# Preparing a bidirectional state-space layer: the step-size chain on 128 rows, the running sums split once, and the input stack and projections by token halves

## The reference

```python
def _mamba3(x, in_proj, conv_w, conv_b, A_log, dt_bias, D, norm_w, out_proj):
    zxbcdt = x @ in_proj
    z, xbc, dt = jnp.split(zxbcdt, [D_INNER, D_INNER + CONV_DIM], axis=-1)
    xp = jnp.pad(xbc, ((0, 0), (K - 1, 0), (0, 0)))
    conv = sum((xp[:, i:i + l, :] * conv_w[:, i] for i in range(K))) + conv_b
    xbc = jax.nn.silu(conv)
    xh, Bm, Cm = jnp.split(xbc, [D_INNER, D_INNER + D_STATE], axis=-1)
    dt = jax.nn.softplus(dt + dt_bias)
    A = -jnp.exp(A_log)
    y = _ssd(xh, dt, A, Bm, Cm) + xh * D[None, None, :, None]
    yg = y.reshape(b, l, D_INNER) * jax.nn.silu(z)
    yn = yg * jax.lax.rsqrt(jnp.mean(yg * yg, -1, keepdims=True) + EPS) * norm_w
    return yn @ out_proj
```

## Time and profile before

| | |
|---|---|
| median of three runs | 698.82 us (697.15 to 700.01) |
| the profiled execution, its own time | 702.39 us |
| its span in the profile | 700.5 us, 1.9 us less than its time |
| busy: PE, ACT, DVE | 495.4, 320.1, 308.5 us |
| xn of the layer complete | about 520.1 us |
| first `near_part` of the forward loop | 548.13 us |
| first `near_part` of the backward loop | 609.26 us |

### The profile page before, as it was taken

One profiled execution on the slowest core, in us unless ns is written; L12 is line 12 of the kernel. 1 busy time (PEld: TensorE's weight loads), 2 busy tenths in 40 slices (PEclk: granted clock), 3 DMA queues, 4 the chain that ended last, 5 costly groups with the idle time before them and its releaser, 6 DMA issues.

```text
span 700.5 us, 10770 instructions
## 1 busy us (share of the span) xinstructions
PE 495.4 (71%) x3956; PEld 274.8 (39%) x3957; DVE 308.5 (44%) x724; ACT 320.1 (46%) x1085; POOL 0.2 (0%) x4
## 2 busy tenths in 40 slices
PE   5654555556987689999855666666576898989633
PEld 2221222223663567677513333333322454455211
DVE  1174000006883678888751000000018896477443
ACT  2232333333672767777633333333335655655411
POOL 0000000000000000000000000000000000000000
PEclk9555555556899899999985555555568999999877
DMA  4000000000000000000000000000024110000000
GB/s 190 0 2 1 0 1 1 0 1 0 2 1 1 0 2 1 1 2 1 1 0 1 0 1 1 0 1 0 1 43 98 39 36 1 1 2 3 0 9 32
DMA packets 9389, 8.37 MB, mean 12 GB/s; under 512 B 3314, under 2 KB 9074, under 8 KB 9204
## 3 DMA queue, kind: packets, MB, share of 16 engines
q1 hardware_dynamic: 9332, 7.62, 3.8%
HBM read 4.99 MB, written 0.52 MB: 8 GB/s over the span
## 4 chain that ended last, share of the span: by engine, by line
PE 58%; DVE 16%; ACT 15%; issue 7%; SPq 1%; DMA 1%; DVEq 1%; ACTq 0%
PE ps L317 16%; ACT arena L335 10%; PE ps L295 4%; PE ps L300 3%; PE ps L620 2%; PE ps L637 2%; PE ps L817 2%; PE ps L781 2%; PE ps L624 2%; DVE arena L1316 2%; PE ps L651 2%; DVE arena L1325 2%; PE ps L796 2%; PE ps L257 2%; PE ps L785 2%
## 5 line engine op out<-in xcount | busy, mean ns | idle before, releaser
L317 PE MATMUL ps<-arena,wsb 16*16 16x16 f32 (+1 forms) x1024 | 131.5, 206 | 116.9 <-ACT arena L335 111.4
L335 ACT ACTIVATE arena<-ps 16x16 f32<-16x16 f32 (+1 forms) x512 | 96.0, 188 | 192.4 <-PE ps L317 192.4
L317 PEld LDWEIGHTS ps<-arena,wsb 16*16 16x16 f32 (+1 forms) x1024 | 76.7, 118 | 200.3 <-ACT arena L335 186.9
L341 DVE TENSOR_TENSOR X<-X,ps 128x128 f32<-128x128 f32 x16 | 4.6, 287 | 199.6 <-PE ps L300 199.5
L1033 ACT ACTIVATE arena<-ps,arena 128x128 f32<-128x128 f32 (+1 forms) x128 | 52.3, 418 | 31.1 <-DVE arena L1317 31.0
L1121 ACT ACTIVATE arena<-ps 128x512 f32<-128x512 f32 x72 | 40.9, 595 | 25.9 <-PE ps L785 20.4
L1467 DVE TENSOR_TENSOR arena<-arena,ps 128x512 f32<-128x512 f32 x64 | 41.8, 682 | 16.0 <-ACT arena L1121 13.6
L1316 DVE TENSOR_REDUCE arena<-ps 128x2 f32<-128x512 f32 (+1 forms) x48 | 33.0, 688 | 18.3 <-PE ps L620 10.9
L637 PE MATMUL ps<-wsb,arena 128*128 128x128 f32 x192 | 30.7, 283 | 11.3 <-DVE arena L1325 11.2
L624 PE MATMUL ps<-arena 128*128 128x256 f32 x128 | 35.4, 400 | 0.0
L1325 DVE TENSOR_TENSOR arena<-arena 128x512 f32<-128x512 f32 x48 | 33.3, 693 | 1.7
(11 more groups left out here) (267 smaller groups left out, 764.5 us busy)
## 6 DMA issues: line engine op xcount, KB each, us to landing
wsb<-weights SPq DMA_DIRECT2D x1, 2060.5 KB, 9.2
arena<-xn SPq DMA_DIRECT2D x16, 128.0 KB, 2.5
arena<-w SPq DMA_DIRECT2D x20, 64.0 KB
wsb<-weights SPq DMA_DIRECT2D x1, 549.5 KB, 4.3
X<-x SPq DMA_DIRECT2D x1, 512.0 KB, 3.4
out<-arena SPq DMA_DIRECT2D x2, 256.0 KB, 2.3
arena<-w_biases SPq DMA_DIRECT2D x20, 17.0 KB
csb<-consts SPq DMA_DIRECT2D x1, 128.0 KB, 9.1
```

The source lines that it names most:

```text
L317: nc.tensor.matmul(step_columns(k, rows, r), w_state, states[0:rows, :, :, t].rearrange("p g j -> p (g j)"), start=False, stop=True, skip_ ...
L335: nc.scalar.activation(states[0:rows, :, :, t + 1].rearrange("p g j -> p (g j)"), step_columns(t // STEP_BANK, rows, t % STEP_BANK), func) ...
```

## The change

Four things change, all in the state-space layer.

1. **The dt chain on 128 rows.** The two token halves go to 64 rows each of one bank, so every instruction of the chain works on 128 x 512 instead of 64 x 1024. The scans become four of 128 rows, and two memsets move ahead of the normalisation. ACT computes the decay rates (`A_log`) ahead of the wait for dt instead of between its exponential and logarithm.
2. **The sums split once.** The cut into three bf16 parts is made for both directions and both halves together, on 128 x 516, into `sum_parts`. `place_sums` copies a direction's rows to their place (six copies). The forward loop keeps one such placement, at step 8, instead of three `decay_part` calls. Six of the eight forward operands are made ahead of the loop, the two others after the fourth `split_b`.
3. **Stack and projections by halves.** The stack is issued as 32 DMAs of half the size: 16 for half 0 behind `normalised` 7, then 16 for half 1 behind `normalised` 8. PE projects x of half 0, turns dt, projects B of half 0, and only then waits for the second set (`M stack rest`); ACT's silu is cut likewise.
4. **Order in the loop's start.** The bank of step n is rotated by two (`ring`); the first CB product is made at step 1; the wait for `M xdt` moves to step 2 and that for the last two operands to step 5.

```diff
+        def place_sums(d):
+            for part in range(3):
+                for h in range(2):
+                    ins = nc.vector.tensor_copy(c3[ROWS * part:ROWS * (part + 1), 2 * h:2 * h + 2],
+                                                sum_parts[E2 * h + ROWS * d:E2 * h + ROWS * (d + 1), part])
+            return ins
...
-            sp.wait_ge(s["normalised"], 8)
-            for i in range(K):
-                for g in range(G):
-                    sp.dma_start(xs[C * i:C * i + C, :, g, K - 1 - i:K - 1 - i + T],
-                                 xn[C * g:C * g + C, :].rearrange("p (j t) -> p j t", j=J)).then_inc(s["M stack"], 16)
+            sp.wait_ge(s["normalised"], 7)
+            for h in range(2):
+                if h == 1:
+                    sp.wait_ge(s["normalised"], 8)
+                for i in range(K):
+                    for g in range(G):
+                        sp.dma_start(xs[C * i:C * i + C, 2 * h:2 * h + 2, g, K - 1 - i:K - 1 - i + T],
+                                     xnj[C * g:C * g + C, 2 * h:2 * h + 2, :]).then_inc(s[("M stack", "M stack rest")[h]], 16)
...
-            pe.wait_ge(s["normalised"], 8)
             for h in range(2):
-                mm = nc.tensor.matmul(ps[0:2 * ROWS, 4 + h, :], W("M_dtW"), halves(xn)[h], start=True, stop=True)
+                pe.wait_ge(s["normalised"], 7 + h)
+                mm = nc.tensor.matmul(ps[E2 * h:E2 * (h + 1), 4, :], W("M_dtW"), halves(xn)[h], start=True, stop=True)
...
+            def project_x_first(h):
+                for gp in range(2):
+                    for gl in range(2):
+                        mm = nc.tensor.matmul(ps[E2 * gl:E2 * (gl + 1), FIRST_X[h][gp], :], wx[:, 0, :],
+                                              xs[:, 2 * h:2 * h + 2, 2 * gp + gl, 0:T], start=True, stop=True)
+                    mm.then_inc(s["M x proj"], 1)
+            def project_bc_first(i, h):
+                for g in range(G):
+                    mm = nc.tensor.matmul(ps[C * g:C * g + C, FIRST_BC[i][h], :], wbc[:, 0, i, :],
+                                          xs[:, 2 * h:2 * h + 2, g, 0:T], start=True, stop=True)
+                mm.then_inc(s["M bc"], 1)
...
             pe.wait_ge(s["M stack"], 16 * K * G)
-            pe.wait_ge(s["M z"], 4)
-            project_x(0)
-            pe.wait_ge(s["M dt"], 1)
-            for jt in range(J * TT):
...
+            project_x_first(0)
+            pe.wait_ge(s["M dt"], 1)
+            for c in range(2 * TT):
+                mm = nc.tensor.matmul(ps[:, 4, c * P:(c + 1) * P], drow[:, 3, c * P:(c + 1) * P],
+                                      W("ident"), is_transpose=True, start=True, stop=True)
+            mm.then_inc(s["M dt turned"], 1)
+            project_bc_first(0, 0)
+            pe.wait_ge(s["M stack rest"], 16 * K * G)
+            pe.wait_ge(s["M z"], 4)
+            project_x_first(1)
+            pe.wait_ge(s["M dt by token"], 1)
+            project_bc_first(1, 0)
+            project_bc_first(0, 1)
+            project_bc_first(1, 1)
...
+            gates(0)
+            for d in range(2):
+                if d == 0:
+                    silu_x_first(0)
+                    act.wait_ge(s["M dt turned"], 1)
+                    nc.scalar.activation(dtt.rearrange("p c h r -> p (c h r)"), ps[:, 4, :], ACT.Copy).then_inc(s["M dt by token"], 1)
+                    silu_bc_first(0, 0, 1)
+                    silu_x_first(1)
+                    silu_bc_first(1, 0, 2)
+                    silu_bc_first(0, 1, 3)
+                    silu_bc_first(1, 1, 4)
...
-            for j in range(J):
-                for q in range(TT):
-                    c0 = j * T + q * P
-                    ins = nc.vector.tensor_tensor_scan(cs[0:rows, j, q, 1:P + 1], drow[0:rows, 1, 0:P], drow[0:rows, 2, c0:c0 + P],
-                                                       0.0, ALU.mult, ALU.add)
+            for c in range(2 * TT):
+                ins = nc.vector.tensor_tensor_scan(cs[:, c // TT, c % TT, 1:P + 1], scan_ones, drow[:, 2, c * P:(c + 1) * P],
+                                                   0.0, ALU.mult, ALU.add)
             link(ins)
             for part in range(3):
-                decay_part(link, 0, part)
-            for k in range(G + HEADS):
+                link(nc.vector.tensor_copy(sum_parts[:, part], cs))
+                if part < 2:
+                    link(nc.vector.tensor_tensor(cs, cs, sum_parts[:, part], ALU.subtract))
+            link(place_sums(0))
+            for k in (0, 1, 4, 5, 6, 7):
                 ins = decay_operand(0, k)
...
+                            for k in (2, 3):
+                                ins = decay_operand(0, k)
+                            ins.then_inc(s["M decay operands"], 1)
                             dve.wait_ge(s["M far sums"], 1)
```

More of the change, by code:

```diff
@@ L225, in hybrid_block, with ring @@
         far_key = wsb[:, first:first + 2 * P].bitcast(BF16).rearrange("p (j r) -> p j r", j=J)
+        def ring(n):
+            return (n + 2) % 4
         def near_unit(k):
@@ L746, in _ @@
                 for i in range(2):
[L747 to L750, removed]
+                    if d == 0:
+                        continue
+                    pe.wait_ge(s["M mean squares saved"] if i == 0 else s["M out saved"], 2 if i == 0 else 1)
                     for h in range(2):
@@ L843, in _ @@
                 for n in range(ALL + 5):
+                    if d == 0 and n == 2:
+                        pe.wait_ge(s["M xdt"], 1)
+                    if d == 0 and n == 5:
+                        pe.wait_ge(s["M decay operands"], 2)
                     if n < ALL:
                         exponent(n)
+                    if n < ALL and (n % SLOTS in (0, 5) and n + d > 0 or n + d == 1 and n == 1):
+                        cb_products(0 if n == 1 else n // SLOTS * DIAG + n % SLOTS - (n % SLOTS > 4))
                     if n == 1:
@@ L1088, in squares, with silu_x_first @@
                 nc.scalar.activation(zf[:, j, :], yg[:, j, :], ACT.Square).then_inc(s["M squares"], 1)
+            def silu_x_first(h):
+                for gp in range(2):
+                    act.wait_ge(s["M x proj"], 2 * h + gp + 1)
+                    nc.scalar.activation(xf[:, 2 * h:2 * h + 2, gp * T:(gp + 1) * T],
+                                         ps[:, FIRST_X[h][gp], :].rearrange("p (j t) -> p j t", j=2), ACT.Silu, bias=W("fwd_bx"))\
+                        .then_inc(s["M x"], 1)
@@ L1090, in _, with silu_bc_first @@
+            def silu_bc_first(i, h, n):
+                act.wait_ge(s["M bc"], n)
+                nc.scalar.activation(halves((bp, cp)[i])[h], ps[:, FIRST_BC[i][h], :], ACT.Silu, bias=W(("fwd_bB", "fwd_bC")[i]))\
+                    .then_inc(s[("M B", "M C")[i]], 1)
             gates(0)
             for d in range(2):
[L1092 to L1101 removed]
@@ L1102, in _ @@
-                if d == 0:
-                    act.wait_ge(s["M dt turned"], 1)
-                    nc.scalar.activation(dtt.rearrange("p a b -> p (a b)"), ps[:, 6, :], ACT.Copy).then_inc(s["M dt by token"], 1)
-                if d == 1:
+                if d == 0:
+                    silu_x_first(0)
[6 more added lines that the diff above has]
+                    silu_bc_first(1, 1, 4)
+                else:
+                    act.wait_ge(s["M y"], J)
+                    for k in range(4):
+                        gp, h = k // 2, k % 2
+                        act.wait_ge(s["M x proj"], 4 * d + k + 1)
+                        nc.scalar.activation(xf[:, 2 * h:2 * h + 2, gp * T:(gp + 1) * T],
+                                             ps[:, k, :].rearrange("p (j t) -> p j t", j=2), ACT.Silu, bias=W("bwd_bx"))\
+                            .then_inc(s["M x"], 1)
@@ L1120, in _ @@
                         act.wait_ge(s["M gram"], count - 2)
[L1121 removed]
+                    nc.scalar.activation(decay[:, n % 3, :], ps[:, ring(n), :], ACT.Exp).then_inc(s["M decay"], 1)
                     if n == 1:
@@ L1505, in _ @@
                         gate(dve, link, d, n // SLOTS - 1)
-                    if d == 0 and n in (8, 10, 12):
-                        decay_part(link, 1, n // 2 - 4)
+                    if d == 0 and n == 8:
+                        dve.wait_ge(s["M decay operands"], 2)
+                        link(place_sums(1))
                     if d == 0 and 20 <= n < 20 + G + HEADS:
```

125 lines of the change are left out of this document (56 added, 69 removed).

## The result

The changed kernel takes 703.22 us (median of 14 runs, 701.08 to 708.58) against 698.01 for the kernel before (14 runs, 693.91 to 702.83): a ratio of **1.008, 95% interval 1.005 to 1.0109**. It is slower by some 5 us. The profiled execution took 706.9 us with a span of 705.1, against 702.39 and 700.5.

What follows compares the result with a forecast made beforehand. SP's stack issuing was taken to bound the path before the projections, and PE the loops. +5.8 us at the first near part and +0.5 for operands gave +6.3 on 698.82, so 705.1 us, 8-in-10 range 697.5 to 707.5.

Steps and rivals of the forecast that it cites:

- The issue interval: On SP's queue, each of the 32 half-size stack issues still takes 0.649 us, so the second set lands at 541.4.
- Rivals A and C: SP's stack issues: A, cost by pieces, 0.325 us, total 692.9, chance 0.17; C, 0.45 plus 0.05 gap, 700.7, chance 0.12.
- The clock: PE idles five us before half 1, begins it at 1.2 GHz and regains full clock 4.4 us later, at 545.9.
- rival B: The clock stays up for PE's second x projections: near part +3.6, total 702.9 us; chance 0.15.
- the sign of being right: At the layer's entry, the first near part starts 5 to 6 us later than before.
- DVE's parts give nothing: Ahead of the forward loop, the shorter dt chain, common split and six operands gain nothing.
- the cover that was named: DVE, done at 541 even at the old length, waits until 548.7 for its first multiplications.
- The operands in the loop: Two operands left for the forward loop's entry take 1.01 us on DVE; cost between 0 and +1.0, taken as +0.5.
- a sign against the earlier trace: A gain inside the forward loop would say DVE had bound it, against the profile rows showing PE busy throughout.
- What follows the forward loop: Behind the forward loop no time was added; the later prefetch of experts, some nine us, holds nothing up.
- The sum: For the whole kernel, 5.8 at the entry and 0.5 from the operands make +6.3 us.

Runs made afterwards that it cites:

- the probe of shapes: The kernel before with 18 extra copies of other shapes behind its stack, each waited for: most issues 465 ns from 128 partitions, 507 from 32.
- g2_before_long: The kernel before with 8 extra matmuls of 512 columns that feed nothing ahead of its wait for the stack: ratio 0.9993 (0.9959 to 1.0026).

## Why the prediction was right

The forecast was 705.1 us and slower (0.70); it is 703.22 and slower. Point by point:

- **The issue interval** was the step that decided, and it held: 538.19 - 519.63 over 29 intervals is 0.640, against 0.649. PE took up the first set at 530.80 (forecast 531.1), and the second had landed at 540.87 (541.4; a landing took 2.04, not 2.2). Rivals A and C needed 0.325 and 0.50; the run with 32 copies and the probe of shapes exclude both. (Of the old issues gives 606 ns as the median, not as an upper bound as the prediction reads it; the sum does not use it.)
- **The clock** had fallen when half 1 came, so rival B is out as well, but it was close: PE idled 3.83 us, not five, and by the row of 540 to 541 the clock was up until 540.1, 0.8 us before the restart. Two sizes were off. It came back at 546.9, 6.0 us after the restart, not 4.4; with that B and C ended at 548.46 instead of 548.1 in spite of the earlier landing. And it fell a second time at 553.7, which no step had: CB took 1.69 us instead of 1.05. Near part at 555.07, forecast 553.9: +6.94 in absolute time and +6.76 from X, where +5.8 stood and 5 to 6 were named as the sign of being right.
- **DVE's parts give nothing**: its wait of 14.90 us is the cover that was named. With the cover gone (16 copies, old order) they are worth 0.7 to 1.2 us at the entry, as far as single executions tell. The operands were ready at 534.25, and not at 531 to 532 as estimated for that case.
- **The operands in the loop**, +0.5: measured 0.49 (38.74 against 38.25), but as the difference of two terms. Built ahead of the loop, it takes 37.84 in three traces. So the operands cost 0.90, and the rest of the change gains 0.41 there, where the prediction held that work taken from DVE gives nothing and named a gain inside the loop as a sign against the earlier trace rows. That 0.5 came out is luck in part. Whether the 0.41 is the split that left the loop or the new order at its start was not taken apart.
- **What follows the forward loop** has no term in the sum, and the loops were to stay of equal length. In this pair of traces the stages behind differ by -1.64, +1.48, -1.72 and -0.95, the first three by falls of the clock. Between the loops the kernel before lost it at the backward projection of x, the changed one did not. Rows of before (588 and 589), then of after (596):

```profile
588.00:589.00 1.00, 1.00 (x32) 0.58 (x20) 0.00 (x0) 0.00 (x0) 0.00 (x0) 0.74 0.00 0
589.00:590.00 1.00, 1.00 (x8) 0.30 (x4) 0.65 (x1) 0.00 (x0) 0.00 (x0) 0.50 0.00 0
```
```profile
596.00:597.00 1.00, 1.00 (x20) 0.43 (x10) 0.51 (x1) 0.00 (x0) 0.00 (x0) 1.00 0.00 0
```

  TensorE had idled 1.86 us before it in the one and 1.44 in the other. That is not the difference: in the run with the old order and 16 copies it idled 1.45 and lost the clock, in g2_before_long 1.85 and kept it. The clock held in all five traces with the order by halves and in one of the nine with the old one. Whether the order causes it, or only shifts where the clock's falls meet the loop's end, was not settled. The backward loop is long in seven of the fourteen, with either order, and in the changed kernel's trace it gave back what was gained between the loops.
- **The sum**: forecast +6.3; 7.25 from entry and forward loop, 4.5 between the two profiled executions with all that the clock did behind, 5.2 between the medians. The mechanism was right; that the entry took 1.0 more than forecast and the total yet 1.1 less is chance as far as is known.

## What to carry to other kernels

A DMA's issue on SyncE's queue had a price that hardly depended on its size (0.47 to 0.61 us here, but for the first in a row), so to cut a row of copies in two doubles the time until the last one is issued (sixteen more took 10 us here). It can pay only where the work behind the first half lasts longer than that. A wait can also cost the clock behind it (3.4 us here): look at what TensorE does ahead of a stage, not only at what the stage waits for. And a gain of 3 us at an entry is smaller than what one execution scatters by (some 9 us here): cut the trace in stages between common events, and let medians of a dozen runs decide.

## What the runs showed of the hardware

- A fetch of instructions among a row of DMAs on SyncE's queue went with one issue of 1.15 to 1.97 us instead of 0.60, in five traces of five; with the fetch elsewhere there was none in nine. In the runs with 18 to 28 extra matmuls of 128 columns ahead of the stack's wait it lay there, in those with eight of 512 it did not. That the fetch holds up the issue is argued from its place, not shown.
- From 128 partitions an issue took 465 ns for 512, 256 and 128 KB alike, from 32 partitions 507 for 128, 64 and 32 KB (the first two of each row aside), and 597 and 606 for 64 and 128 KB in a row without waits.
- Two queues, SyncE's and GpSimd's, moved 64 KB copies of 32 partitions at a mean of 209 and 215 GB/s, where one got 97; but the ratios of both versions that used GpSimd's queue lie above what entry and forward loop say, by 1.9 and 3.6 us, the first hardly beyond its interval.
- TensorE's idle time ahead of a stage did not by itself tell whether the clock fell there: 1.45 us went with a fall, 1.44 and 1.85 with none.
